# Tiles of gathered rows for a two-layer edge-attention GNN, collected by ScalarE and SP beside GpSimd

## The reference

```
f     = (x @ W_ni.T)[src] + (x @ W_nj.T)[dst] + e @ W_fij.T
f     = leaky_relu(f, 0.2)
score = f @ attn
a     = exp(score - segment_max(score, dst)[dst])
a     = a / segment_sum(a, dst)[dst]
h_out = segment_sum((x @ W_node.T)[src] * a[:, None], dst)
```

## Time and profile before

| | |
|---|---|
| Median of 3 runs (lowest, highest) | 2189.23 us (2187.99, 2191.67) |
| The profiled execution's own time | 2185.84 us |
| Its span, first to last instruction | 2184.0 us |
| Granted TensorE clock, mean | 0.929 of full speed |
| PE busy | 1812.9 us, 83% |
| PEld busy | 1243.9 us, 57% |
| VectorE busy | 1497.5 us, 69% |
| ScalarE busy | 421.8 us, 19% |
| GpSimd busy | 1588.6 us, 73% |
| DMA | 486.65 MB, mean 223 GB/s |

### The profile page before, as it was taken

One profiled execution on the slowest core, in us unless ns is written; L12 is line 12 of the kernel. 1 busy time (PEld: TensorE's weight loads), 2 busy tenths in 40 slices (PEclk: granted clock), 3 DMA queues, 4 the chain that ended last, 5 costly groups with the idle time before them and its releaser, 6 DMA issues.

```text
span 2184.0 us, 43046 instructions
## 1 busy us (share of the span) xinstructions
PE 1812.9 (83%) x10541; PEld 1243.9 (57%) x10696; DVE 1497.5 (69%) x5518; ACT 421.8 (19%) x844; POOL 1588.6 (73%) x1671
## 2 busy tenths in 40 slices
PE   5699889888888888888857788888788888878887
PEld 3366666555565666555634555555555555555566
DVE  6488888777777767777735666666666667657666
ACT  2221121111111111111111112222212222222221
POOL 7777777777777777777277777777777777777771
PEclk9899999998999889999979999999999999999988
DMA  9889998888888878888456666666666666666661
GB/s 318 258 269 279 281 288 279 260 251 250 266 253 259 253 244 263 258 255 255 141 172 189 192 200 196 195 198 196 192 199 195 195 193 200 194 189 203 195 198 44
DMA packets 349544, 486.65 MB, mean 223 GB/s; under 512 B 114284, under 2 KB 215188, under 8 KB 349454
## 3 DMA queue, kind: packets, MB, share of 16 engines
q1 hardware_dynamic: 236515, 248.47, 37.7%
q0 software_dynamic: 78752, 213.75, 33.7%
q10 hardware_dynamic: 34203, 23.55, 3.6%
HBM read 407.69 MB, written 81.38 MB: 224 GB/s over the span
## 4 chain that ended last, share of the span: by engine, by line
POOL 54%; issue 18%; PE 14%; DMA 6%; DVE 5%; ACTq 1%; POOLq 1%; DVEq 1%; ACT 0%; SPq 0%
POOL xsrc L516 54%; PE pair L761 4%; PE bSC L750 4%; PE pair L719 2%; DMA xsrc<-h_table,idx_slot 2%; DMA xsrc<-x_table,idx_slot 2%; DMA proj<-xsrc 2%; PE pair L730 1%; ACTq L551 1%; DVE amat L1055 1%; PE pair L734 1%; DVE fT L1168 1%; DVE h L1171 0%; PE pair L722 0%; PE bXT L795 0%
## 5 line engine op out<-in xcount | busy, mean ns | idle before, releaser
L516 POOL DMA_INDIRECT xsrc<-h_table,idx_slot x831 | 792.4, 954 | 295.8 <-issue 249.6
L516 POOL DMA_INDIRECT xsrc<-x_table,idx_slot x767 | 731.4, 954 | 234.5 <-issue 226.7
L622 ACT ACTIVATE zc<-pair 128x512 f32<-128x512 f32 x416 | 248.4, 597 | 1584.2 <-PE pair L734 1004.8
L719 PE MATMUL pair<-edge_in,wts 128*128 128x512 f32 x832 | 483.8, 665 | 18.6 <-DMA window<-proj 18.4
L730 PEld LDWEIGHTS pair<-ident,xsrc 128*128 128x128 f32 x1600 | 195.8, 149 | 527.9 <-DMA xsrc<-h_table,idx_slot 294.4
L750 PE MATMUL bSC<-fT,attn_at 128*32 128x128 f32 x3328 | 480.3, 292 | 17.2 <-issue 3.9
L1168 DVE TENSOR_TENSOR fT<-pair,zc 128x512 f32<-128x512 f32 x416 | 285.6, 687 | 267.7 <-ACT zc L622 266.7
L730 PE MATMUL pair<-ident,xsrc 128*128 128x128 f32 x1600 | 273.7, 297 | 234.4 <-DMA xsrc<-h_table,idx_slot 162.2
L761 PEld LDWEIGHTS pair<-amat,xsrc 128*128 128x128 f32 x3328 | 426.5, 198 | 63.2 <-issue 50.8
L761 PE MATMUL pair<-amat,xsrc 128*128 128x42 f32 x3328 | 458.9, 290 | 2.5 <-DVE amat L1051 2.3
L750 PEld LDWEIGHTS bSC<-fT,attn_at 128*32 128x32 f32 x3328 | 350.8, 116 | 112.4 <-issue 96.4
(11 more groups left out here) (148 smaller groups left out, 1273.2 us busy)
## 6 DMA issues: line engine op xcount, KB each, us to landing
edge_in<-eT SPq DMA_DIRECT2D x208, 256.0 KB
rel_bc<-relrow_g SPq DMA_DIRECT2D x416, 128.0 KB
h1T<-h SPq DMA_DIRECT2D x208, 256.0 KB
edge_in<-h1T SPq DMA_DIRECT2D x208, 256.0 KB
window<-proj SPq DMA_DIRECT2D x416, 32.0 KB
xsrc<-h_table,idx_slot POOLq DMA_INDIRECT x831
xsrc<-x_table,idx_slot POOLq DMA_INDIRECT x767
hx<-xT SPq DMA_DIRECT2D x48, 121.0 KB
```

The source lines that it names most:

```text
L516: pool.indirect_dma_start(xsrc[b][:, i, 0:width], None, table, bass.IndirectOffsetOnAxis(ap=idx_slot[b][:, i:i + 1], axis=0)).then_inc(L.g ...
L622: nc.scalar.mul(zc[s][:, :], bZ[s][:, :], SLOPE).then_inc(L.z_scaled, 1)
L719: mm(bZ[s][:, :], fij, edge_in[q][:, :], start=True, stop=False)
```

## The change

In each layer each of seven turns has tiles that GpSimd no longer gathers. They are the last tiles of chunk 5, 8, ..., 23, that is of slot 7 of xsrc2: in layer 1 the last tile (BY_ACT), in layer 2 the last two (BY_ACT and BY_SP). Their rows are fetched one by one, with plain DMAs of one row of 1 KB, whose address comes from a register, into a staging tile; the complete staging tile is then copied to its place in xsrc2 with one DMA.

- In layer 1 ScalarE fetches rows 0 to 63 of the tile and SP rows 64 to 127, into the same staging tile; ScalarE copies it.
- In layer 2 ScalarE fetches one tile of 128 rows and SP another, each into a staging tile of its own, and each copies its own.
- The row numbers come in two new inputs: idxR has the 128 indices of the BY_ACT tiles, idxQ those of the BY_SP tiles. A line of 128 is loaded into SBUF per turn, and read into registers, a slot's share at a time.
- The shares: ScalarE 2 to 4 rows a slot in layer 1 and 5 to 7 in layer 2 (ROWS_AT), SP 3 and 6 (SP_ROWS), from slot 3 on in 21 slots of 24.
- TensorE waits for the copies before the z-sum of slot 7 of those chunks, and for three or two gathers in place of four.
- ScalarE's loop is now written over turns of three chunks. The windows of four groups share two tiles in SBUF, to make room; in the narrow path each group still has a place of its own.

```diff
+AIDED = (CH - XB) // XB
+AID_AT = 2 * XB - 1
+HALF = P // 2
+ROWS_AT = {1: [2, 3, 2, 4, 4, 3, 3, 3], 2: [5, 7, 5, 6, 7, 6, 6, 7]}
+ACT_ROWS = {1: HALF, 2: P}
+SP_ROWS = {1: (HALF, 3), 2: (0, 6)}
+SP_BEGIN = 3
+SP_SLOTS = 3 * GC - SP_BEGIN
+BY_ACT, BY_SP = TC - 1, TC - 2
+AIDED_TILES = {1: 1, 2: 2}
@@ GpSimd
-                        for i in range(g * TG, g * TG + TG - (SHORT if ends else 0)):
+                        aided = not isinstance(c, int) and b == AID_AT % XB and g == GC - 1
+                        for i in range(g * TG, g * TG + TG - (SHORT if ends else aided * AIDED_TILES[L.n])):
@@ SP, at the end of each slot
+                        if aid is not None:
+                            aided_rows(L, *aid, c, g)
+            def aided_rows(L, turn, u, c, g):
+                if turn == 3 and g == 1:
+                    if L.n == 2 and reached(u, 1):
+                        sp.wait_ge(L.sp_rows_in, u * (16 * P))
+                        sp.wait_ge(L.num_made, c * GC - 2 * GC)
+                        sp.dma_start(xsrc[AID_AT % XB][:, BY_SP, :], sp_stage[:, :]).then_inc(L.sp_aided_in, 16)
+                    if not isinstance(u, int) or u < AIDED:
+                        sp.dma_start(sp_line[:, :], (idxR if L.n == 1 else idxQ)[bass.ds(u, 1), :]
+                                     ).then_inc(L.sp_line_in, 16)
...
+                if turn == 0 and g == SP_BEGIN:
...
+                    above(sp, L.aided_in if L.n == 1 else L.sp_aided_in, u * 16)
+                    sp.wait_ge(L.sp_line_in, u * 16 + 16)
+                _, rows = nc.values_load_multi_w_load_instructions(
+                    sp_line[0:1, at:at + count], engines=(SP_,), min_val=0, max_val=N - 1,
+                    skip_runtime_bounds_check_because=IN_RANGE)
+                to = stage if L.n == 1 else sp_stage
+                for p, row in enumerate(rows):
+                    sp.dma_start(to[at + p:at + p + 1, :], L.table[bass.ds(row, 1), :]).then_inc(L.sp_rows_in, 16)
@@ ScalarE, at the end of each slot
+                def aided_rows(turn, u, begins, c, g):
+                    if turn == 2 and g == GC - 3 and begins:
+                        act.dma_start(line[:, :], idxR[bass.ds(u + 1, 1), :]).then_inc(L.line_in, 16)
+                    if turn == 2 and g == GC - 2 and reached(u, 0):
+                        act.wait_ge(L.rows_in, u * (16 * ACT_ROWS[L.n]) + 16 * ACT_ROWS[L.n])
+                        if L.n == 1:
+                            act.wait_ge(L.sp_rows_in, u * (16 * HALF) + 16 * HALF)
+                        act.wait_ge(L.num_made, c * GC - GC)
+                        act.dma_start(xsrc[AID_AT % XB][:, BY_ACT, :], stage[:, :]).then_inc(L.aided_in, 16)
...
+                    for p, row in enumerate(rows):
+                        act.dma_start(stage[at + p:at + p + 1, :], L.table[bass.ds(row, 1), :]).then_inc(L.rows_in, 16)
@@ TensorE, z_sum
+                        if b == AID_AT % XB and g == GC - 1:
+                            above(pe, L.aided_in, rounds * 16)
+                            if L.n == 2:
+                                above(pe, L.sp_aided_in, rounds * 16)
+                            pe.sem_inc(pe_passed, 1)
+                            earlier = (L.uses_before[b] + 1) * (16 * TG) - 16 * AIDED * AIDED_TILES[1] * (L.n - 1)
+                            pe.wait_ge(L.gathered[b][g], rounds * (16 * (TG - AIDED_TILES[L.n])) + earlier)
```

More of the change, by code:

```diff
@@ L29, with act_rows, sp_rows @@
 SHORT = NT - TILES
+AIDED = (CH - XB) // XB
+AID_AT = 2 * XB - 1
+IN_RANGE = "src lies in [0, N)"
+HALF = P // 2
[6 more added lines that the diff above has]
+AIDED_TILES = {1: 1, 2: 2}
+def act_rows(n, turn, g):
+    counts = ROWS_AT[n]
+    before = 0 if turn == 0 else counts[GC - 1] + (turn - 1) * sum(counts)
+    at = before + (0 if turn == 0 else sum(counts[0:g]))
+    return at, max(0, min(counts[g], ACT_ROWS[n] - at))
+def sp_rows(n, turn, g):
+    first, count = SP_ROWS[n]
+    k = turn * GC + g - SP_BEGIN
+    if k < 0 or k >= SP_SLOTS:
+        return 0, 0
+    return first + k * count, P - (first + k * count) if k == SP_SLOTS - 1 else count
 class Layer:
@@ L173, in program @@
         edge_in = [sb(f"edge_in{g}", [P, W]) for g in range(GS)]
-        window = [sb(f"window{g}", [P, 3 * TG, P], bf16) for g in range(GS)]
+        window = [sb(f"window{g}", [P, 3 * TG, P], bf16) for g in range(GS // 2)]
+        stage = sb("stage", [P, 2 * P])
+        line = sb("line", [1, P], i32)
+        sp_stage = sb("sp_stage", [P, 2 * P])
+        sp_line = sb("sp_line", [1, P], i32)
         rel_bc = [sb(f"rel_bc{g}", [P, W], bf16) for g in range(GS)]
@@ L398, in first_nodes, with chunk @@
                     return first
-                def chunk(c, idx_to):
+                def chunk(c, idx_to, aid=None):
                     if narrow:
@@ L616, in layer, with slot @@
             def layer(L, narrow):
-                def slot(c, g, front, soft):
+                def slot(c, g, front, soft, aid):
                     n, s = c * GC + g, g % 2
@@ L637, in slot @@
                         copy_rows(n + 1, 1 - s)
+                    if aid is not None:
+                        aided_rows(*aid, c, g)
+                def aided_rows(turn, u, begins, c, g):
[7 more added lines that the diff above has]
+                        act.dma_start(xsrc[AID_AT % XB][:, BY_ACT, :], stage[:, :]).then_inc(L.aided_in, 16)
+                    if turn == 2 and g == GC - 1 and begins:
+                        above(act, L.aided_in, u * 16 + 16)
+                        act.wait_ge(L.line_in, u * 16 + 32)
+                        act.sem_inc(act_passed, 1)
+                    turn, begun = (0, begins) if turn == 2 and g == GC - 1 else (turn + 1, reached(u, 0))
+                    at, count = act_rows(L.n, turn, g)
+                    if not begun or count == 0:
+                        return
+                    _, rows = nc.values_load_multi_w_load_instructions(
+                        line[0:1, at:at + count], engines=(ACT_,), min_val=0, max_val=N - 1,
+                        skip_runtime_bounds_check_because=IN_RANGE)
+                    for p, row in enumerate(rows):
+                        act.dma_start(stage[at + p:at + p + 1, :], L.table[bass.ds(row, 1), :]).then_inc(L.rows_in, 16)
                 def copy_rows(n, s):
@@ L642, in copy_rows, with turn @@
                     nc.scalar.copy(xsT[s][:, :], bXT[:, :]).then_inc(L.xt_copied, 1)
-                def turn(c, front, soft):
+                def turn(c, front, soft, aid=None):
                     for g in range(GC):
-                        slot(c, g, front, soft)
+                        slot(c, g, front, soft, aid)
                 def whole_slab(k):
@@ L733, in z_sum @@
                     if narrow:
-                        last = mm(bZ[s][:, :], window[q][:, 0, :], onehot[s][:, :], start=False, stop=True)
+                        last = mm(bZ[s][:, :], window[q % 2][:, q // 2, :], onehot[s][:, :], start=False, stop=True)
                     else:
@@ L737, in z_sum @@
                             for part in range(3):
-                                mm(bZ[s][:, i * P:i * P + P], window[q][:, 3 * i + part, :],
+                                mm(bZ[s][:, i * P:i * P + P], window[q % 2][:, 3 * i + part, :],
                                    onehot[s][:, i * P:i * P + P], start=False, stop=False, skip_group_check=True)
```

66 lines of the change are left out of this document (52 added, 14 removed).

## The result

The changed kernel takes 2274.69 us (median of 5 runs, 2273.17 to 2278.92) against 2189.06 (2187.99 to 2191.67): a ratio of 1.0392, 95% interval 1.0377 to 1.0406. It is slower by 86 us; forecast were 2167 us and a range up to 2197. The mean granted TensorE clock of the profiled execution is 0.888 in place of 0.929.

What follows compares the result with a forecast made beforehand. GpSimd's gathers, one per 1.25 us, were taken as the bound; 26.3 us saved less some 4 given back made 2163.4 on the profiled 2185.8, plus 3.4 for the median: 2167 us. Its own range was 2161 to 2174, eight-in-ten 2160 to 2197.

Steps and rivals of the forecast that it cites:

- What bounds the kernel: Both layers: GpSimd's gathers, one per 1.25 us, set the pace and the other engines follow.
- the ceiling: GpSimd, both layers: 21 gathers fewer save at most 26.3 us, 8.8 in layer 1 and 17.5 in layer 2.
- SP in layer 2: SP's queue in layer 2: its turn takes 114.3 us against GpSimd's 117.5, so it fits with 3% left.
- SP in layer 1: SP's queue in layer 1: 93 of 118.8 us a turn, so nothing is late.
- ScalarE: ScalarE's queue: fullest layer 2 chunk 34.4 us of 39.2, lateness absorbed by slack; layer 1 easy.
- The DMA engines: Both layers: busiest engine's share rises to some 0.91 and 0.80; only gathers, a few tenths later in layer 1.
- The sum: Whole kernel: 26.3 us at the ceiling, some 4 us given back for late slots, giving 2167 us.
- A: Layer 2: SP becomes the bound, its turn 126 us, total 2207 to 2222 us, slower; chance 0.17.
- B: Layer 2: ScalarE is late at 0.58 us a row, layer 2 gains nothing, about 2183 us; chance 0.06.
- C: Layer 1: gathers land later on busy DMA engines, about half the gain lost, 2176 us; chance 0.12.
- D: PE's own chain is as near as GpSimd's; freed time becomes GpSimd's waits on PE, near 2189 us; chance 0.05.
- three signs of being wrong: Row issues 0.5 us or more apart; PE's waits moving to window and edge loads; GpSimd waiting tens of us for PE.

Runs made afterwards that it cites:

- the table: 23 different register loads put on SP in layer 2 of the kernel before, between single-row DMAs, on the slow chip; read from distances, no time given.
- aligned eights: Changed kernel with SP reading its row numbers eight at a time from multiples of eight, same rows and engines: 2160.99 us, 0.9872 of the kernel before.
- its own experiment: Kernel before with only ScalarE's seven tiles of layer 2 taken from GpSimd, none collected by SP, layer 1 unchanged: 2182.59 us, 0.9957.
- the run without register loads: Changed kernel with SP's row numbers made from its loop counter, so other rows but as many were fetched: 2162.19 us, 0.9879 of the kernel before.
- the experiment with whole tiles: Kernel before with ScalarE alone collecting seven whole tiles in each layer, SP none: 2218.64 us, 1.0127.

## Why the prediction was wrong

**What bounds the kernel** was right, and so was the ceiling. Where SP keeps up, 21 gathers less are worth 27.2 us (2188.14 - 2160.99), against 26.3 computed.

**SP in layer 2** is the step that failed, and in it one term: "The register load of six lies between nothing and 0.9 us (6/8 of 1.19); I take 0.6". It costs 1.24 in the mean, above the upper end. One of SP's turns in layer 2, from the jump at 1644.9 us to the next, each part with the steps up to the next instruction, us:

| part | computed | in the trace |
|---|---|---|
| three loads of each slot | 37.4 | 39.0 |
| indices, destinations, slab | 4.7 | 5.0 |
| three loads of eight window bases | 3.6 | 2.5 |
| the staged copy and the row of indices | 1.0 | 1.1 |
| 128 rows | 55.0 | 55.4 |
| 21 loads of row numbers | 12.6 | 25.1 |
| jump back | nothing | 3.0 |
| semaphore and register steps | nothing | 1.8 |
| the turn | 114.3 | 132.9 |

Two thirds of what was missing is the one term. The jump back was priced for ScalarE and not for SP; SP's jumps in the kernel before took 0.2 to 0.3 us and gave no sign of it. The row itself, 0.43 us, was right.

**Why the bound was none.** The prediction says that the register load isn't in the trace as a row, and that no row shows the load alone. It is there. SP's load of eight window bases and VectorE's load of eight node numbers in the kernel before, ns min/median/max:

```profile
L395 SPq TENSOR_LOAD <-part_row x52: 520/531/1177, 65.1 to 2087.3; - x52
L1074 DVEq TENSOR_LOAD <-group_row x54: 546/1855/3137, 101.9 to 2165.2; - x54
```

Eight numbers both, 0.53 us and 1.85. In chunk c SP's load starts at number 8c, VectorE's at 8c - 14, two past a multiple of four. So the two rows hinted at the price of the start before anything was built, though other things differ between two engines. The 1.19 us was not VectorE's load but its mean idle time in layer 1 ahead of the one-hot; layer 2's mean, 40.8 / 22 = 1.85, is as long as the load itself, and the prediction uses it for ScalarE. As an estimate, 6/8 of 1.85 is 1.39 us, and SP's turn would have been 131 us. SP's own row alone would have misled: it is below the 0.6 that was taken. Why that load of eight takes 0.70 us in the changed kernel (L433) and 0.53 before is open.

**SP in layer 1** failed by the same term: "93 of 118.8 us. Nothing is late there". A load of three was put at 0.3 us. The turn from 535.9 us, 123.7 us long, has 26.3 us of them where 6.3 were computed, 3.8 for the jump, 53.9 for the four issues of a slot where 50 were taken, 29.4 for the rows where 27.5 were, and 10.3 for the rest where 9 were. Alignment doesn't explain the loads here: by the table three numbers cost 1.14 us of gap from a multiple of four and 1.19 from elsewhere, against the mean of 1.52. The scatter above that is layer 1's; aligned eights too take 1.04 us in the mean there and 0.72 in layer 2. What lengthens them is open.

**ScalarE** was right for layer 2 in what it did to the time, by its own experiment, and half a tile in layer 1 is harmless, by the eights. But its register loads were put at 0.6 us as well and last 1.44. The fullest chunk is then 41 us of work and not 34.4, over the 39.2 that it has: here the forecast was saved by the overlap, and in part by luck. The sign that was named, a growing wait of fT for zc, didn't come (133.9 us against 136.4). **The DMA engines** were right in that they cost nothing, as the run without register loads shows. The share that was expected to rise to some 0.91 and 0.80 on the busiest engine is 0.86 and 0.70 in the mean of all in the run with the eights, against 0.85 and 0.68. **The sum** thus failed by SP alone; with the loads at their true price the same working gives 127 us a turn, with the jump too 130.

**The rivals.** A is what happened, given 0.17, with the right mechanism, the wrong layer count and a wrong culprit in its price (0.52 us a row). It named 2207 to 2222 for layer 2 alone; SP alone in layer 2 gave 2243. Beside it stood an estimate of 1.2 us for six registers, by the figure for each register of the Trainium skill, "Runtime: NRT & Kernel Launch", section "Instruction fetch mechanics", which made the turn 127 us. It was nearer to the truth than what I took. The table has 0.21 us for each number of an unaligned load, and a fixed part besides. What B feared came true only in the experiment with whole tiles, and in layer 1. C and D did not occur. Two of the three signs of being wrong came, the waits for the windows and GpSimd's for PE; the third, rows 0.5 us apart, didn't, since it watched the wrong price. The mistake in the chances was that the forecast rested on 3% of room with a sum whose range, 85 to 132, reached over the limit by 15 us and below it by 32.

## What to carry to other kernels

Give the sequencer that issues DMAs its own budget, slot by slot, register loads and loop jumps included, before work is moved to it: it shows as idle in a table of busy times and is the bound all the same. Read register values in aligned groups of four, eight or twelve and hold them over several slots; here that alone turned 3.9% slower into 1.3% faster, on the usual chip; on the slow one the same kernel was 6.8% slower than the kernel before was there. Ask the trace for the sequencer's instructions by their line before a term is called unseen: they are not in the table of busy times and not in the timeline. A term that can decide should be given its worst nearby price in the likeliest case when the margin is a few per cent, and layer by layer.

## What was not expected of the hardware

- A register load on SP added some 0.33 us and 0.21 us a step between two DMAs, a step being one number, or four from a multiple of four (gaps of 0.78 us for four of them, 1.30 for four from elsewhere, with 0.19 that are not the load's). In layer 1 of the changed kernel loads of three took 1.30 us in the mean, and why is open.
- The jump back of SP's loop left the sequencer without work for 2.5 to 3.5 us in the changed kernel, with 564 and 683 instructions in the body, and for 0.2 to 0.3 in the one before, with 344 and 266.
- A one-row DMA with an address in a register took 0.43 us of SP, against 0.52 to 0.54 for one of 128 rows.
- On one chip the kernels of this study were 30 to 41% longer (the kernel before 2851.29 us in place of 2188, at a granted clock of 0.785 in place of 0.93), with waits of up to 41 us on ScalarE that nothing in the profile explains. What slowed that chip was not looked into.
